# A fused LayerNorm, attention and ternary feed-forward kernel: deferring pass-B transposes, staggering the LayerNorm tiles, and five pass-A units a chunk

## What is computed

```python
xn = layernorm(x)                                  # no affine part
qkv = xn @ w_qkv                                   # 2048 -> 3 * 2048
scores = (q / sqrt(128)) @ k.T                     # causal
s = softmax(scores) @ v, then @ w_out
scale = mean(abs(w)); wq = sign(w) * (abs(w) >= 0.7 * scale)   # for w1 and w2
h = gelu(xn @ w1_q.T + b1)                         # 2048 -> 8192
g = silu(h @ w2_q.T + b2)                          # 8192 -> 2048
out = x + s * g
```

## Time and profile before

| | |
|---|---|
| median of three executions | 5418.09 us (5404.64 to 5702.88) |
| profiled execution | 5396.88 us |
| its span, core 0, the slowest | 5395.2 us (other cores 5325.2 to 5389.5) |
| PE matmul busy | 3892.2 us, 72% |
| VectorE (DVE) busy | 1266.9 us, 23% |
| ScalarE (ACT) busy | 1170.7 us, 22% |
| DMA | 767 MB, mean 142 GB/s |
| mean granted TensorE clock, core 0 | 0.831 |

### The profile page before, as it was taken

One profiled execution on the slowest core, in us unless ns is written; L12 is line 12 of the kernel. 1 busy time (PEld: TensorE's weight loads), 2 busy tenths in 40 slices (PEclk: granted clock), 3 DMA queues, 4 the chain that ended last, 5 costly groups with the idle time before them and its releaser, 6 DMA issues.

```text
span 5395.2 us, 50992 instructions; the slowest of 8 cores (5325.2 to 5395.2 us)
## 1 busy us (share of the span) xinstructions
PE 3892.2 (72%) x19720; PEld 1744.7 (32%) x20033; DVE 1266.9 (23%) x1179; ACT 1170.7 (22%) x1675; POOL 283.0 (5%) x463
## 2 busy tenths in 40 slices
PE   3477757666667777775343425898999899899997
PEld 2222222222223333332122212343344344334443
DVE  5344433333333323323223231000000000010001
ACT  2232312222333333333112221120011001101200
POOL 0000000000000000000001001000000000010001
PEclk7687877777777777776676757899999999999999
DMA  4677656665433433333667677645655564566455
GB/s 124 149 162 156 148 107 131 132 121 124 109 99 77 109 93 78 95 96 95 162 170 183 164 189 172 172 151 173 172 162 167 160 179 157 158 172 172 141 147 161
DMA packets 1082030, 767.08 MB, mean 142 GB/s; under 512 B 251522, under 2 KB 1054659, under 8 KB 1077187
## 3 DMA queue, kind: packets, MB, share of 16 engines
q1 hardware_dynamic: 942916, 596.02, 42.4%
q0 software_dynamic: 138880, 167.80, 13.1%
HBM read 688.24 MB, written 109.05 MB: 148 GB/s over the span
## 4 chain that ended last, share of the span: by engine, by line
PE 56%; DMA 25%; DVE 10%; ACT 4%; issue 4%; SPq 1%; DVEq 0%; ACTq 0%; POOL 0%; POOLq 0%
DMA BIGB<-w 20%; PE P L948 16%; PE P L992 15%; PE P L467 7%; DMA XNB<-w2t 4%; PE P L820 3%; PE P L493 3%; PE P L400 3%; DVE WP L388 3%; DVE WACC L322 3%; PE PROW L711 2%; ACT BIGB L410 2%; PE P L719 2%; PE P L736 2%; DVE WP L382 2%
## 5 line engine op out<-in xcount | busy, mean ns | idle before, releaser
L992 PE MATMUL P<-XNB,XNT 128*128 128x512 bf16 x4016 | 918.4, 386 | 115.4 <-DMA XNB<-w2t 82.0
L948 PE MATMUL P<-BIGB 128*128 128x512 bf16 x4012 | 881.7, 379 | 19.0 <-DMA BIGB<-w1t 14.5
L400 PE MATMUL P<-IDENTB,WP 128*128 128x128 bf16 x2048 | 241.9, 291 | 672.9 <-DVE WP L388 465.3
L992 PEld LDWEIGHTS P<-XNB,XNT 128*128 128x128 bf16 x4096 | 402.0, 99 | 631.2 <-issue 182.4
L948 PEld LDWEIGHTS P<-BIGB 128*128 128x128 bf16 x4096 | 401.0, 98 | 500.2 <-issue 18.0
L750 ACT ACTIVATE XNB<-P,NEGM 128x512 bf16<-128x512 f32 x640 | 428.3, 687 | 598.6 <-DVE P L745 324.5
L467 PE MATMUL P<-XNT,WQB 128*128 128x512 bf16 x1991 | 477.5, 400 | 12.9 <-ACT XNT L575 6.8
L1030 DVE TENSOR_TENSOR WQB<-P,WQB 128x512 f32<-128x512 f32 x64 | 41.2, 686 | 1822.3 <-PE P L992 1813.5
L711 PE MATMUL PROW<-XNB,ONESCB 128*1 128x512 bf16 x640 | 310.6, 485 | 180.0 <-ACT XNB L750 173.4
L400 PEld LDWEIGHTS P<-IDENTB,WP 128*128 128x128 bf16 x2048 | 185.0, 130 | 741.9 <-issue 741.2
L410 ACT COPY BIGB<-P 128x1024 bf16<-128x1024 bf16 x256 | 259.1, 1012 | 677.7 <-PE P L400 677.7
(11 more groups left out here) (71 smaller groups left out, 1571.4 us busy)
## 6 DMA issues: line engine op xcount, KB each, us to landing
BIGB<-w SPq DMA_DIRECT2D x256, 1024.0 KB, 9.2
BIGB<-w1t SPq DMA_DIRECT2D x64, 2048.0 KB, 9.1
XNB<-w2t SPq DMA_DIRECT2D x512, 256.0 KB, 3.2
w1t<-BIGB POOLq DMA_DIRECT2D x16, 2048.0 KB, 8.1
XNT<-dotd SPq DMA_DIRECT2D x64, 512.0 KB, 6.0
w2t<-BIGB POOLq DMA_DIRECT2D x64, 512.0 KB, 7.3
WQB<-wqkv POOLq DMA_DIRECT2D x48, 512.0 KB, 18.6
BIGB<-x SPq DMA_DIRECT2D x16, 1024.0 KB, 6.0
```

The lines of the kernel that those rows point to most:

```text
L400: lambda e, pv=pview, o=oslot, rr=rr, j=j: e.transpose(pv[:, j * 128:(j + 1) * 128], qout_slot(o)[:, (rr * 8 + j) * 128: (rr * 8 + j + 1) ...
L948: lambda e, b=bank, p=psl, dt=dt, fl=fl: e.matmul(P[b][:], w1p_slot(p)[:, dt * 512 + fl * 128: dt * 512 + (fl + 1) * 128], xnc_d(dt), star ...
L992: e.matmul(P[gb][:], XNT[:, f * 512 + tt * 128: f * 512 + (tt + 1) * 128], w2m_dslot(m)[:, fh * 512:(fh + 1) * 512], start=(f == 0), stop= ...
```

## The change

Four things are edited.

1. `emit_passB` is split. What follows the VectorE passes (transposes, copies, the write) becomes `passB_stage2`, and a call carries it out for the unit before, held in `st["B_pend"]`, ahead of the new unit's load and VectorE passes.
2. The LayerNorm loop is split: the load, the statistics and rstd of tile t are issued ahead of the normalisation, transposes and copies of tile t-1.
3. `finalize_scale` moves from the start of heads 4 and 8 to behind NEGM in heads 5 and 8.
4. `emit_passA(4)` becomes `emit_passA(5)`.

```diff
+        st["B_pend"] = None
+
+        def passB_stage2(ent):
+            ui, mat, pnl, ch, oslot, r2 = ent
+            pslot = pnl % 2
+            evacs = []
+            pview = P7.bitcast(BF16)
+            for rr in range(2):
+                for j in range(8):
+                    w = ([r2, st["p7f"]] if j == 0 else [])
+                    kb.op("tensor",
+                          lambda e, pv=pview, o=oslot, rr=rr, j=j: e.transpose(
...
+                evc = kb.op("scalar",
...
+                            ae, 1, waits=[tdone, st["qpanel_war"][pslot]])
+                st["p7f"] = evc
+                evacs.append(evc)
+            if mat == 0 and ch == 3:
+                wr = kb.op("gpsimd",
...
+            st["qout_war"][oslot] = (pe, pe.n)
+
         def emit_passB(nmax, pA_read):
             for _ in range(nmax):
+                if st["Bi"] >= len(units) and st["B_pend"] is None:
+                    return
+                if st["B_pend"] is not None:
+                    passB_stage2(st["B_pend"])
+                    st["B_pend"] = None
                 if st["Bi"] >= len(units):
-                    return
+                    continue
                 mat, pnl, ch = units[st["Bi"]]
...
                 st["qin_war"][islot] = r2
-                evacs = []
-                pview = P7.bitcast(BF16)
-                for rr in range(2):
...
-                st["qout_war"][oslot] = (pe, pe.n)
+                st["B_pend"] = (ui, mat, pnl, ch, oslot, r2)
                 st["Bi"] += 1
...
-        for t in range(NT):
+        ln_a2 = {}
+
+        def emit_ln_stats(t):
             s = t % 4
-            s2 = t % 2
...
+            ln_a2[t] = a2
+
+        def emit_ln_finish(t):
+            s = t % 4
+            s2 = t % 2
             v4 = kb.op("vector",
...
-                       ve, 1, waits=[a2, xnb_war[s2]])
+                       ve, 1, waits=[ln_a2[t], xnb_war[s2]])
...
             if t % 4 == 3:
                 emit_qkv_block(0, t // 4)
+            return last
+
+        for t in range(NT):
+            emit_ln_stats(t)
+            if t >= 1:
+                lnt_last_evac = emit_ln_finish(t - 1)
+        lnt_last_evac = emit_ln_finish(NT - 1)
...
         for h in range(H):
             hs = h % 2
-            if h == 4 and st["s_done"][0] is None:
-                prow_rd = finalize_scale(0, prow_rd)
-            if h == 8 and st["s_done"][1] is None:
-                prow_rd = finalize_scale(1, prow_rd)
...
             st["p7f"] = negm_ready
+
+            if h == 5 and st["s_done"][0] is None:
+                prow_rd = finalize_scale(0, prow_rd)
+            if h == 8 and st["s_done"][1] is None:
+                prow_rd = finalize_scale(1, prow_rd)
...
                 if h >= 8:
                     emit_passB(2, pA_read)
                 else:
-                    emit_passA(4)
+                    emit_passA(5)
...
         emit_passB(len(units), pB_read)
         assert st["Bi"] == len(units), f"passB incomplete {st['Bi']}"
+        assert st["B_pend"] is None, "passB pend not flushed"
```

More of the change, by code:

```diff
@@ L363, in finalize_scale @@
             return a1
+        st["B_pend"] = None
[9 more added lines that the diff above has]
+                          lambda e, pv=pview, o=oslot, rr=rr, j=j: e.transpose(
+                              pv[:, j * 128:(j + 1) * 128],
+                              qout_slot(o)[:, (rr * 8 + j) * 128:
+                                           (rr * 8 + j + 1) * 128],
+                              IDENTB[:]),
+                          pe if j == 7 else None, 1 if j == 7 else 0,
+                          waits=w)
+                tdone = (pe, pe.n)
+                base = (ch * 2048 + rr * 1024) if mat == 0 else (rr * 1024)
+                evc = kb.op("scalar",
+                            lambda e, pv=pview, psl=pslot, b=base: e.copy(
+                                qpanel_slot(psl)[:, b:b + 1024], pv[:]),
+                            ae, 1, waits=[tdone, st["qpanel_war"][pslot]])
[3 more added lines that the diff above has]
+                wr = kb.op("gpsimd",
+                           lambda e, p=pnl, psl=pslot: e.dma_start(
+                               out=dw1t[:, p * 8192:(p + 1) * 8192],
+                               in_=qpanel_slot(psl)),
+                           s_w1t[pslot], 16, waits=evacs)
+                st["qpanel_war"][pslot] = wr
+                st["w1t_done" + str(pslot)] = wr
+            elif mat == 1:
+                wr = kb.op("gpsimd",
+                           lambda e, p=pnl, psl=pslot: e.dma_start(
+                               out=dw2t[:, p * 2048:(p + 1) * 2048],
+                               in_=qpanel_slot(psl)[:, 0:2048]),
+                           s_w2t[pslot], 16, waits=evacs)
+                st["qpanel_war"][pslot] = wr
+                st["w2t_done" + str(pslot)] = wr
+            st["qout_war"][oslot] = (pe, pe.n)
@@ L374, in emit_passB @@
                 oslot = ui % 2
-                pslot = pnl % 2
                 v = kb.op("sync",
@@ L558, in build_nc @@
                            ALU.subtract, ALU.mult),
-                       ve, 1, waits=[a2, xnb_war[s2]])
+                       ve, 1, waits=[ln_a2[t], xnb_war[s2]])
             xf_war[s] = v4
+            last = None
             for rr in range(2):
@@ L582, in build_nc @@
                 pA_read[rr] = ev
-                lnt_last_evac = ev
-            lnt_tile_done[t] = lnt_last_evac
-            xnb_war[s2] = lnt_last_evac
+                last = ev
+            lnt_tile_done[t] = last
+            xnb_war[s2] = last
             if t % 4 == 3:
                 emit_qkv_block(0, t // 4)
+            return last
[4 more added lines that the diff above has]
+        lnt_last_evac = emit_ln_finish(NT - 1)
         xnt_ready = lnt_last_evac
```

## The result

The changed kernel took 5267.07 us (median of 9, 5251.77 to 5574.53) where the kernel before, over ten executions by now, took 5488.02; the ratio is 0.9698 with a 95% interval of 0.9647 to 0.9749, in which executions with a lower granted clock on one die are left out on both sides. So it is 3.0% faster (2.5 to 3.5), and 3.7% had been forecast, measured against the mean of 5406.5. The profiled execution took 5251.77 us, span 5250.2, against 5396.88 and 5395.2.

The account below looks back on a forecast made before the run. Loads of w lead the chain; attention heads and projection before 3437 us can move, the feed-forward part not. Terms -13 + 93 - 37 - 119 - 124 = -200 from 5406.5 give 5206 us, range 5150 to 5260.

Parts of the forecast that it names:

- Part 1: LayerNorm pipeline: VectorE's 0.79 us wait for ScalarE's rstd goes, 16 times; -13 us.
- Parts 2 and 3: Heads 0 to 7: five pass-A units a chunk cost +93 us; thresholds behind NEGM remove stalls, -37.
- Part 4: Heads 8 to 15: deferred pass-B transposes no longer wait for VectorE's passes; 31 x 3.85 = -119 us.
- the rival that the clock stays up: Pass-B blocks in heads: without the idle 3.97 us PE keeps full clock; 90 us more, 5116; chance 0.10.
- the rival's other half: Clock in heads with pass B: 9 matmuls behind each block also get faster, 0.18 us each.
- Part 5: Output-projection tiles: deferred transposes shorten 40 w2 units by 3.1 us each, -124.
- I take 10.0: Projection: time of a w2 unit beside a tile after deferral, 10.0 us instead of 13.1.
- the 13 us that was to be its sign of being wrong: Projection tiles: a unit still taking 13 us would show the forecast wrong.
- the 24 units without tiles stay: Projection: w2 units without a tile keep 8.3 us each, a loop of load and passes over two slots; change 0.
- The rival that transfers are the limit, wholly or half: Projection tiles: DMA transfers bind, deferral there gains near nothing, 5330 us, or half, 5268; chance 0.15.
- halfway: Projection tiles: the case where transfers are the limit only in part; 5268 us in all.
- The page's bandwidth that the prediction weighed: Projection tiles: HBM limit near 358 GB/s, 5.9 us a unit would do, the loop's 8.7 decides, -176.

Follow-up runs that it names:

- The undoing: The changed kernel with four pass-A units a chunk again instead of five: 5106.9 us, ratio 0.9496 to the kernel before.
- the two experiments above: On the changed kernel, four w2 load slots with loads issued two units ahead: 16 tiles 169.5 and 176.3 us; half of each w2 unit loaded: 110.2 and 116.6.
- four slots: The changed kernel with four load slots for w2 in pass B, loads issued two units ahead: tiles 169.5 and 176.3 us, units alone 98.5 and 98.9.
- the second run of the kernel: The changed kernel once more, unaltered, as reference for three further kernels: 5264.4 and 5268.3 us, feed-forward part 1936.0.

## Why the prediction was right, and where it was wrong

**Part 1, LayerNorm, right.** -14.5 measured, -13 forecast. The wait of 0.79 in the earlier trace rows is gone: it was 14.0 us in 16 waits on core 0, and VectorE now starts the normalisation at the end of the statistics, without a bracket.

```profile
113.43 0.08 DVE L554 DVE_READ_ACCUMULATOR BIGB<-BIGB,LNS 128x1 f32 x1
113.43 1.34 DVE L573 TENSOR_SCALAR BIGB<-BIGB,LNS 128x2048 bf16<-128x2048 f32 x1
```

**Parts 2 and 3, pass A in fives and the thresholds, right.** +55.7 against +56. Head by head the forecast's 145, 163, 169, 128 and 106 stand beside 144 and 146, 162, 164 and 166, 122 and 103 on the mean of the cores. The undoing gave +91 for the fifth unit where +93 stood. That the two together agree to a microsecond is luck: the same code took 1155.6 to 1187.0 us for these heads in different executions, and the move of the thresholds alone gave -26 over the whole stretch, -40 in heads 3 and 7. That a load more in each chunk is paid in full, and that a head without pass A still needs some 103 us, carried this.

**Part 4, deferral in the heads, right in kind, too small.** 155.1 became 136.9 a head on the mean of the cores, 18.2 instead of 15.4. A block in the changed kernel, PE's timeline, beside the earlier trace rows:

```profile
1714.44 0.39 PE L745 MATMUL P<-XNB,QKVB 128*128 128x512 bf16 x1
1714.67 0.61 PE L376 MATMUL P<-IDENTB,WP 128*128 128x128 bf16 x8
1716.89 0.61 PE L376 MATMUL P<-IDENTB,WP 128*128 128x128 bf16 x8 [1.61 <-ACT BIGB L386]
1718.90 0.61 PE L376 MATMUL P<-IDENTB,WP 128*128 128x128 bf16 x8 [1.40 <-DVE WP L436]
1720.81 1.01 PE L376 MATMUL P<-IDENTB,WP 128*128 128x128 bf16 x8 [1.30 <-ACT BIGB L386]
```

PE's wait for VectorE in seven heads, where the kernel before has 107.8 us in 28 waits:

```profile
PE P L376 <- DVE WP L436: 33.0, 22, 3.5
```

The 3.97 is gone, and the second unit is ready when the first pair is done: what is left are nearly all waits like the one of 1.40 here, where the copy would hold PE for 1.3 anyway. Three of the four groups run at the full 2.4 GHz level, 0.61 us. In the 28 blocks of heads 8 to 14 before, on core 0, the first group did so in 11 (the earlier trace rows shows one of them) and the others never; now, on core 3, the first three do in 21 of 27. So of the 126.6 us by which these heads shortened between the two slowest cores, 96 are waits of the transposes, less than the 104 forecast, about 21 the shorter groups, and the rest lies elsewhere. The 21 are a part of the rival that the clock stays up, and they explain most of the excess over the forecast; the granted clock of heads 8 to 14 rose from 0.77 to 0.82. The matmuls behind the block still run at 1.2 GHz, nine in 4.00 us, so the rival's other half did not come. Core 3, behind the block above:

```profile
1722.00:1726.00 4.00, 4.00 (x9) 0.62 (x9) 0.57 (x1) 2.89 (x4) 0.00 (x0) 0.50 1.03 317
```

**Part 5, deferral in the projection, the step that failed.** The term was 40 x 3.1 = -124; it measured -51, and -47 within one chip. The mechanism was right in that the loop over two units opened and the transfers took over as the limit, which the two experiments above show. What failed is the size: "I take 10.0" for a unit beside a tile, which came to 11.2 and 11.5 on the mean of the cores. Of the 73 us that are missing, this is 43.

The 10.0 is 8.3 us of engine time at a share of 0.83. Both were off, the first more. The 8.3 came from core 0, the slowest, with a share of 0.63; the mean of the cores before is 0.68 and 0.69 over 12.5 and 12.8 us a unit, which is 8.5 and 8.8. With the deferral it is 0.80 and 0.79 over 11.2 and 11.5, 8.9 and 9.1. The packets show where the time went: those of 512 bytes, which are the w loads, took 36.9 ns each in the first tile stretch before and 40.1 afterwards, those of 256 bytes 18.3 and 19.2 (means of the cores). The share of 0.83 was above the 0.79 of the earlier trace rows, and the forecast's own 10.4 for 0.79 was the better number. The share did come out near 0.8, as the prediction said it would, and a unit did not take the 13 us that was to be its sign of being wrong: neither sign could tell 10.0 from 11.3.

Another 14 us are the starting value: 13.1 is core 0's, and on the mean of the cores there were only 12.5 and 12.8 to shorten. 10 us were given back in the units alone, costed at nothing ("the 24 units without tiles stay"), and 6 are missing at the end. With four slots the units alone are back at 98.5 with about the same share, so it is not a lack of engine time.

The rival that transfers are the limit, wholly or half, given 0.15, was the right one. That its "halfway" put 5268 us and 5267.07 was measured is luck: it allowed for 62 us missing in the projection, where 73 are, and heads 8 to 14 gave 23 us more than the forecast it starts from.

The page's bandwidth that the prediction weighed, the Trainium skill (DMA: Bandwidth & Descriptors, Where 436 GB/s comes from), would have had transfers out of the way. The runs decide against it for this pattern: the stretches with full loads above move 170 to 202 GB/s, and the one with half loads 240.

**The sum.** -200 forecast, -140 on the mean of the cores: +73 from part 5, -23 from heads 8 to 14, +5 from head 15, -2 from the LayerNorm part, and +8 in the feed-forward part, which the second run of the kernel shows to be spread. The total came nearer than its parts, since the excess in the heads hid a third of what the projection lacked.

## What to carry to other kernels

When a wait is removed from a loop, ask of every queue in it how much room it has left. Here SP waited for PE in 125 of 210 us, which looked like slack, and its own issues, which grew from 70 to 153 us, used it up. Cost a stretch that will be bound by transfers at the highest busy share of the DMA engines that any stretch shows, not above it, and expect more engine time for the same bytes: here a share of 0.79 to 0.84 with full loads, and 3 to 5% more engine time a unit. These are numbers of this mix of loads; with half loads the share was 0.87. Take the starting value from the mean of the cores and not from the slowest one when the cores differ. Where the loads stand in the order matters more than how many are asked for at once: the 128 loads of pass A cost 91 us more in fives than in fours beside the chunks, and with some of them behind the projection blocks the same heads took 232 us less than in fives.

## What the runs showed of the hardware

- An issue on SP is not of fixed length: the same otst2 load takes 0.52 us to issue in the kernel before and 1.6 to 6.3 us in the changed one, the same w load 0.37 us where little else is under way and up to 10.5 beside tiles in the changed kernel. The issues are then themselves a serial resource: in the tiles the landing, counted from the issue, does not grow with four slots (17.3 us against 17.1 with two on the same chip). That a full queue holds the issue is the likely reading, and no run here tests it alone. Nor do the runs tell whether the DMA engines or the memory behind them set the 170 to 202 GB/s of the stretches with full loads.
- Halving the bytes of the w2 loads took a unit beside a tile from 11 to 6.9 us, more than in proportion to the whole traffic (2.1 to 1.6 MB a unit). The share of the DMA engines was 0.87 on the mean of the cores, above that of any stretch with full loads, and a packet of 512 bytes took 35.5 ns, less than with full loads (36.9 before, 40.1 in the changed kernel). So the time of a packet does not simply follow the share.
- Executions differ where transfers set the pace, and less elsewhere: identical code took 1155.6, 1157.3 and 1161.6 us for heads 0 to 7 in three runs on one chip and 1182.7 and 1187.0 in two other runs, but 958.4 to 959.0 for heads 8 to 14 in four of them, and 1936.0 to 1942.9 for the feed-forward part.
